# Sixteen landed columns and paired relation products in the first edge pass, and tables split by ScalarE and VectorE in turns

## The reference, cut to what matters

```python
h = relu(layernorm(x))
q = h @ Wq_part + ...                       # one row per node
key_of_edge = K[src] + R[etype]             # K: table of node keys, R: 64 relation rows
score = sum_over_head(q[dst] * key_of_edge) / 4
w = exp(score - max_over_edges_of(dst))
x = x + (sum(w * v[src]) / (sum(w) + 1e-8)) @ Wo + bo
```

## Time and profile before

| | us |
|---|---|
| median of 3 runs | 8024.5 |
| the profiled execution | 8015.14 |
| its span | 8013.4 |
| TensorE matmul busy | 2909.3 (36%) |
| VectorE busy | 4677.0 (58%) |
| ScalarE busy | 1435.1 (18%) |
| GpSimd busy | 3668.7 (46%) |
| granted TensorE clock, mean | 0.691 |

### The profile page before, as it was taken

The page is one execution under the profiler, slowest core; times in us unless marked ns, Lnnn a source line. Parts: engine busy times, 40 slices in busy tenths (PEclk is TensorE's granted clock), DMA queues, the critical chain, the costliest instruction groups (busy, mean ns, idle before and its releaser), DMA issues. The chain is left out here.

```text
span 8013.4 us, 112882 instructions
## 1 busy us (share of the span) xinstructions
PE 2909.3 (36%) x28649; PEld 2368.4 (30%) x28650; DVE 4677.0 (58%) x10839; ACT 1435.1 (18%) x3773; POOL 3668.7 (46%) x4402
## 2 busy tenths in 40 slices
PE   4189633455555523344223432345200000001344
PEld 3168512344444422243223431334200000000122
DVE  9677345566666646687567764677544444444333
ACT  0123100111111112222112221344311111110000
POOL 0155224443333324565445544544466666563655
PEclk9999986676777766677566765666655555555677
DMA  0034223344434423345334443334332231222334
GB/s 21 10 92 108 58 75 96 96 105 101 101 88 96 92 59 70 80 83 77 67 75 83 84 69 64 77 74 73 53 51 51 52 52 51 49 51 55 77 83 80
DMA packets 293996, 576.70 MB, mean 72 GB/s; under 512 B 137262, under 2 KB 182043, under 8 KB 273827
## 3 DMA queue, kind: packets, MB, share of 16 engines
q0 software_dynamic: 113232, 255.82, 21.2%
q1 hardware_dynamic: 142642, 278.18, 11.3%
q10 hardware_dynamic: 38049, 41.86, 1.7%
HBM read 479.10 MB, written 29.32 MB: 63 GB/s over the span
## 5 line engine op out<-in xcount | busy, mean ns | idle before, releaser
L2992 PE MATMUL bank<-tab,oh 128*128 128x136 bf16 x11700 | 906.9, 251 | 704.3 <-PEq L2984 383.6
L2992 PEld LDWEIGHTS bank<-tab,oh 128*128 128x128 bf16 x11700 | 876.7, 113 | 765.2 <-issue 765.2
L1422 PE MATMUL bank<-ident,hid 128*128 128x128 f32 x125 | 55.8, 446 | 2622.7 <-PEq L1421 1482.1
L1422 PEld LDWEIGHTS bank<-ident,hid 128*128 128x128 f32 x125 | 22.7, 181 | 2669.4 <-issue 2669.4
L2735 POOL DMA_INDIRECT land_a<-table,idx_a x624 | 653.5, 1047 | 228.4 <-issue 166.4
L2754 POOL DMA_INDIRECT land_r<-table,idx_r x492 | 507.5, 1031 | 215.5 <-issue 148.4
L2915 ACT ACTIVATE rows<-bank 128x408 f32<-128x408 f32 x936 | 398.0, 514 | 848.6 <-ACTq L2914 640.2
L2841 DVE TENSOR_TENSOR prod<-prod 128x128 f32<-128x128 f32 (+4 forms) x621 | 536.5, 864 | 14.6
L2571 PE MATMUL bank<-tab_l,oh_l 128*128 128x128 bf16 x3846 | 407.5, 241 | 222.1 <-PEq L2534 102.0
L2827 DVE TENSOR_TENSOR prod<-rows,bank 128x5376 f32<-128x5376 f32 x75 | 431.6, 5755 | 61.1 <-DVEq L2826 30.5
L3218 PE MATMUL bank<-tab_l,oh_l 128*128 128x384 bf16 x1250 | 263.8, 381 | 454.9 <-PEq L3212 333.3
(11 more groups left out here) (515 smaller groups left out, 8530.2 us busy)
## 6 DMA issues: line engine op xcount, KB each, us to landing
loc<-el_loc SPq DMA_DIRECT2D x78, 1088.0 KB
loc_l<-el_loc SPq DMA_DIRECT2D x52, 1088.0 KB
typ_l<-el_typ SPq DMA_DIRECT2D x52, 672.0 KB
rows_r<-land_r SPq DMA_DIRECT2D x123, 272.0 KB
landings_l<-landings_l SPq DMA_DIRECT2D x41, 784.0 KB
attr<-in_edge_attr ACTq DMA_DIRECT2D x75, 343.8 KB
land_a<-table,idx_a POOLq DMA_INDIRECT x936
land_r<-table,idx_r POOLq DMA_INDIRECT x492
```

What stands on the lines that cost most here:

```text
L2992: last = pe.matmul(got[g % full][:, (c - of[0]) * W1:(c - of[0] + 1) * W1], oh[:, o], tab[:, t, x], start=n == 0, stop=n == len(parts) - 1 ...
```

## The change

1. In the first edge pass the eight wide columns are no longer made by products. The lists keep their node numbers (`el_ovf` grows by `NW` words), and GpSimd gathers them along with the eight landed ones: `LAND` = 16 gathers into `land_a`. The on-chip one-hots shrink to 26 columns (`FC`).
2. Relation products go in pairs of columns. `oht[c // 2]` has the first column's one-hot on partitions 0 to 63 and the second's on 64 to 127; `rel3[:, x]` (three parts) is block diagonal, 256 columns wide. Three products of 256 columns serve two key columns, where four of 128 did. The list stage makes the paired order with one more small VectorE instruction a run.
3. Key groups: four landed, two narrow of four, three narrow of four, three of two (still 12). Value groups: 12 of two or three columns, 26 in all (34 before).
4. In all five passes with a table ScalarE makes the high and the middle casts and VectorE the two subtractions, the second of which writes the low part as bf16 (no third cast). `whole` has three buffers, `rest` two. In the convolutions ScalarE does its casts between its copies of the first round's PSUM groups.

The diff, cut to its core (the convolutions and the last pass have the same `act_split` and `split_table`):

```diff
+            TH = MC // 2
+            FC = NB + 1
+            LAND = MC - FC
-            wide = [range(c, min(c + 4, PC)) for c in range(NB + 1, PC, 4)]
-            narrow = [range(c, c + 4) for c in range(NB - 7, NB + 1, 4)] + [range(c, c + 3) for c in range(0, NB - 7, 3)]
+            narrow = [range(c, c + 4) for c in range(FC - 8, FC, 4)] + [range(c, c + 4) for c in range(6, FC - 8, 4)] + [range(c, c + 2) for c in range(0, 6, 2)]
+            landed_groups = [range(c, c + HALF) for c in range(FC, MC, HALF)]
+            key_groups = landed_groups + narrow
+            VG = 2 * len(banks)
+            value_groups = [range(FC * (n - 1) // VG, FC * n // VG) for n in range(VG, 0, -1)]
...
+            def act_high(act, g):
+                act.wait_ge(s(f"whole_in{g % 3}"), 16)
+                act.sem_inc(s(f"whole_in{g % 3}"), -16)
+                act.activation(tab_of(g)[:, :, 0], whole_of(g), ACT.Copy).then_inc(s("high_ready"), 1)
+            def act_middle(act, g):
+                act.wait_ge(s("rest_ready"), 1)
+                act.sem_inc(s("rest_ready"), -1)
+                act.activation(tab_of(g)[:, :, 1], rest_of(g), ACT.Copy).then_inc(s("middle_ready"), 1)
+            def act_split(act, n):
+                for g in range(n + 2 if n else 0, min(n + 3, len(tiles))):
+                    act_high(act, g)
+                for g in range(n + 1 if n else 0, min(n + 2, len(tiles))):
+                    act_middle(act, g)
...
-                        for c in range(FIRST):
+                        for c in range(LAND):
                             pool.indirect_dma_start(land_a[:, c, :], None, source, ...
...
-                    def split(g, m):
...
+                    def split_rest(g):
+                        dve.wait_ge(s("high_ready"), 1)
+                        dve.sem_inc(s("high_ready"), -1)
+                        dve.tensor_tensor(rest_of(g), whole_of(g), tab_of(g)[:, :, 0], ALU.subtract).then_inc(ch.semaphore, ch.one())
+                        dve.wait_ge(ch.semaphore, ch.count)
+                        dve.sem_inc(s("rest_ready"), 1)
+                        dve.sem_inc(s(f"whole_free{g % 3}"), 1)
+                    def split_low(g):
+                        dve.wait_ge(s("middle_ready"), 1)
+                        dve.sem_inc(s("middle_ready"), -1)
+                        dve.tensor_tensor(tab_of(g)[:, :, 2], rest_of(g), tab_of(g)[:, :, 1], ALU.subtract).then_inc(ch.semaphore, ch.one())
+                        dve.wait_ge(ch.semaphore, ch.count)
+                        dve.sem_inc(s("tab_ready"), 1)
+                    def split_table():
+                        split_rest(0)
+                        for g in range(len(tiles)):
+                            if g + 1 < len(tiles):
+                                split_rest(g + 1)
+                            split_low(g)
...
-                    def type_rows(c, to, first, last):
-                        for x in range(2):
-                            done = pe.matmul(to, oht[:, c], rel3[:, x], start=first and x == 0, stop=last and x == 1, ...)
-                        return done
+                    def type_rows(n, of):
+                        for c in range(of[0], of[0] + len(of), 2):
+                            for x in range(3):
+                                pe.matmul(keys_of(n)[:, c - of[0]:c - of[0] + 2], oht[:, c // 2], rel3[:, x], start=c == of[0] and x == 0, stop=False, ...)
```

More of the change, by code:

```diff
@@ L2126, in _ @@
                 def _(sp):
-                    for k in range(2):
+                    for k in range(3):
                         sp.sem_inc(s(f"whole_free{k}"), 1)
@@ L2293, in split_relations @@
+                        dve.wait_ge(ch.semaphore, ch.count)
+                        for mine, k in halves:
+                            dve.tensor_copy(rel3[mine, 2, k], total[mine, 0:D]).then_inc(ch.semaphore, ch.one())
                         dve.wait_ge(ch.semaphore, ch.count)
@@ L2407, in _ @@
                     onehots()
-                    for g, m in enumerate(tiles):
-                        split(g, m)
+                    split_table()
                     for name in ["land_r_free", "rows_r_free"]:
@@ L2508, in _ @@
                     act.sem_inc(s("own_free"), 16)
-                    take_landed(0)
+                    for n in range(len(tiles)):
+                        act_split(act, n)
+                        if n == 3:
+                            take_landed(0)
                     runs_of_block(0)
@@ L2874, in _ @@
                     onehots()
-                    for g, m in enumerate(sizes):
-                        split(g, m)
+                    split_table()
                     if number == 1:
@@ L3199, in _ @@
                         dve.sem_inc(s(name), -1)
+                @block.scalar
+                def _(act):
+                    for n in range(len(sizes)):
+                        act_split(act, n)
                 @block.tensor
```

247 lines of the change are left out of this document (140 added, 107 removed).

## The result

The changed kernel takes 8134.09 us (median of four runs, 8128.61 to 8139.82) against 8022.66 us for the kernel before: ratio 1.0146, interval 1.0131 to 1.0161. It is slower by 1.5%, where 7835 us was forecast. The profiled execution took 8129.86 us, its span is 8128.1.

The account below looks back on a forecast made before the run. The end of GpSimd's gather burst, beside which TensorE nearly stops, was taken to set each run. From 8015.1 us, -66 (one-turn runs), -60 (others) and -58 (tables) gave 7831, median about 7840; 7835 taken, range 7680 to 8005.

Parts of the forecast that it names:

- What bounds the kernel now: First edge pass: the end of GpSimd's gather burst sets the run of 59.2 us, not the amount of matmul work alone.
- The burst's start and length: GpSimd's gathers start 5.2 us later, 13.2 us after the source one-hots; sixteen take 21.2 us, the turn's end at 46.
- What TensorE does by then: TensorE beside the `land_a` gathers: node update, then 81 second key products, done 34 us after the source one-hots.
- rival B: Longer burst catches the second keys in its `land_a` part: +2.5 us in 15 runs, +3 in 10; 8035 to 8050; chance 0.12.
- the O+47.9 of the sum: One-turn run: TensorE's stall ends 47.9 us after the source one-hots are ready, 1.9 us behind the last gather.
- -6 for these runs: The ten runs of more turns in the first edge pass: -6 us each from shorter values, -60 in all.
- VectorE: First edge pass: narrower one-hots and weighings save 2.1 us a run, counted in the sum; as its own term 0 to -52.
- Tables: Table filling in the passes: casts split between ScalarE and VectorE, -58 us in sum, -22 of it in the first pass.
- further bound of +36: Slower case with ScalarE's doubled copy out of `land_a` holding the gathers, +27 us: +36 instead of +9 in all.
- Rival A: TensorE's stalls do not grow with the gathers, or move where nothing waits; a run follows its work: -365, 7660; chance 0.24.

Follow-up runs that it names:

- the pauses: Small GpSimd copies between gathers, first-kind chip, against the kernel before: one in the changed kernel 0.9971; with tables, pairs and the early list, one short 0.9716, three 0.9583.
- the early list: SyncE loads the list ahead of the landed turn's copy instead of behind it: 0.9931 in the kernel before (first kind), 0.9964 in the changed kernel (second kind).

## Why the prediction was wrong

- *What bounds the kernel now*: right for this chip. TensorE's keys wait for the end of the burst, and the pauses show that this sets the run: with them one-turn periods fall from 63.2 to 55.0 us, and from 59.5 to 51.0 and 45.2, though GpSimd has more to do (the early list in the last two left one-turn runs as they were in the kernel before, 58.0 against 58.2). The trace could not tell that another chip has no hold.
- *The burst's start and length*: begins at O+10.9 (O+13.2 forecast), ends at O+41.7 (O+46). Gathers are 1.28 us apart on average, 416 in all, as forecast. The start is 2.3 us sooner than forecast. 1.5 of them are the landed groups, read by O+9.3 instead of O+10.8: the last two took 1.5 to 1.7 us each, not 2.62, at a granted clock of 1.00.
- *What TensorE does by then*: **this step failed.** It let 81 second keys through in the `land_a` part at the pace of the first window of the earlier trace rows and had them done at O+34, before the turn. The node update did end at O+20 (2307.7). But 17 us into the burst the stream was held: 36 of the loads from 2310.9 on passed by 2316.0, 7 in the next 17.9 us, and the rest of the keys came after the last gather. In the window that I trusted, the first 11 us of a row, the hold had not begun. Cut at the right place, the trace of before shows it (TensorE's weight loads by window, the row of gathers goes from 1894.1 to 1915.2):

```profile
1894.00:1901.00 7.00, 2.29 (x10) 0.50 0.89 246
1901.00:1905.00 4.00, 3.71 (x41) 0.60 0.99 234
1905.00:1916.00 11.00, 0.92 (x9) 0.62 0.55 125
```

  41 loads pass in 4 us, and 9 in the next 11. Taken whole, that window has 51 loads in 11 us, 4.6 per us, which is no more than rival B's 4.5; I had divided its busy time by the count (0.118 us) and so left the idle part out. In the rows of before and after the pace falls with the time since the row began, and I had read it as belonging to a kind of gather; the row behind the pause shows that this time is not all that counts. It is rival B's place and its consequence, keys caught in the `land_a` part, with 0.12 of the chance. B's even rate is not what happened: B had 16 of the 81 keys left after the last gather, and 39 were.
- *The size*: B had +2.5 us for one-turn runs and +3 for the others. Measured: 63.2 - 58.2 = +5.0 and +10.5. The release comes 4.5 us behind the last gather (1.9 assumed), but the burst ends 4 us sooner than forecast, so TensorE is let go at O+46.2, near the O+47.9 of the sum. What is longer lies behind it, 18.1 us to the next O where the forecast had 6.9 and B 13.8: 39 keys, their reduction and shift, and all the values. In the two-turn runs the burst starts 23 to 24 us after the one-hots in both traces, and the last gather is issued 10 us later than before, so there the eight gathers are paid in full. I had -6 for these runs, from shorter values alone.
- *VectorE*: source one-hots 1.08 us, relation ones 0.92, landed weighing 2.42, 47 us less busy over the stage (2.1 us a run were forecast): right and worth nothing, as it waits.
- *Tables*: -58 forecast, 22 of them in the first pass. Away from it the stages give 35.7 + 12.6 + 4.5 = 53 us, more than the 36 forecast there. Within the first pass the tiles take 2.85 instead of 5.5 us, 24 us in nine, but the first period falls by 9.5 us only (87.6 to 78.1). Alone the tables gave 44.6 us on the second kind.
- *Slips in the working*, none of which decides it: the two early narrow groups have 12 double products, not 6 (the trace of after shows x6 in each); by its own rows the burst would end at O+45.2, not O+46; nine tiles of 5.5 us make 49.5, not 46; and rival B with its further bound of +36 reaches 8060, not 8050.
- *Rival A* describes the second kind of chip as far as products beside gathers go: there 116 loads pass. The rule of the Trainium skill that stands beside it ("SBUF — State Buffer", "Who interferes with whom": TensorE never waits on anyone, which is said of memory ports) agrees with the second kind. The first kind shows something else, 7 loads in 17.9 us, and whether a port has to do with it no run shows. Even on the second kind the changed kernel loses 1%, mostly through GpSimd's ring, which no rival of mine had.

## What to carry to other kernels

Moving work from a busy engine to an engine in a ring (here gather, copy, list, gather) is paid where the ring binds, however much the busy engine saves: on the second kind the eight gathers cost 10.1 us in each of the ten and 2.5 in the others. Follow the ring once round before the sum is made. When a stream of instructions stops for "issue" beside a long row of another engine's DMA work, look at where in the row it begins before a rate is taken from a window, and try to break the row: on the first kind three pauses of 2 us brought one-turn runs to 45.2 us, where fewer products alone left them at 59.5. And measure on more than one chip before such a pause is kept: on the second kind it takes back all that tables and pairs give (1.0005 against 0.9906).

## What the hardware showed beyond expectation

Chips of one type differ by 7.4% on the same kernel (8022.66 and 7430.36 us), although casts and gathers last equally long: medians of 577 ns for a cast and 0.95 us for a gather in both. Nearly 60% of the difference lies in the first edge pass (1747.6 against 1404.2 us between the tables' first casts). On the chips of the first kind it is the instruction stream and not a product that is slow: single products last 0.22 to 0.37 us with 1.0 to 2.6 us before them, at distances near multiples of 0.7 us (1.42, 2.10, 2.80), and VectorE's instructions come with 0.7 us of "issue" in the burst too. The hold sets in step by step. Over all rows of gathers of the first edge pass in the trace of before, "issue" ahead of products takes 0.01 of the time in the first 3 us of a row, 0.16 and 0.29 in the next two stretches of 3 us, 0.38 and 0.75 in the two after; in the kernel before on the second kind it is 0.00 in all of them. What in these chips makes the difference, and whether it is the fetching of instructions that the gathers hold, stays open; no run here could show it.
